# An attention and low-rank layer pair on one core: bulk loads behind the query stack, one-piece query split by way of DRAM, key copy and prologue on other engines

## The reference

```python
# x [2, 2048, 1024]; Wq, Wo [1024, 1024]; Wkv [1024, 64]; 32 heads of 32, one shared key/value head; float32
q  = (x @ Wq).reshape(b, s, 32, 32)
kv = x @ Wkv;  k, v = kv[..., :32], kv[..., 32:]
scores = einsum('bqhd,bkd->bhqk', q, k) * 32 ** -0.5
scores = where(causal, scores + slopes[:, None, None] * (pos_k - pos_q), -inf)      # ALiBi slopes
attn = einsum('bhqk,bkd->bqhd', softmax(scores), v).reshape(b, s, 1024) @ Wo
h = layernorm(x + attn)
# second layer: dense W [1024, 1024] and bias, plus a low-rank product whose rank (8, 16, 32 or 64)
# is that of the largest of four gate scores, taken row by row
out = layernorm(h + h @ W.T + bias + (h @ A[:r].T) @ B[:, :r].T)
```

## Time and profile before

| | |
|---|---|
| median of 3 runs | 3603.31 us (3599.54 to 3610.43) |
| the profiled execution | 3600.88 us, its span 3599.1 us |
| PE, DVE, ACT, POOL busy | 95%, 64%, 51%, 44% of the span |
| mean granted TensorE clock | 0.97 of full |
| DMA | 148.32 MB, mean 41 GB/s |

### The profile page before, as it was taken

One profiled execution on the slowest core, in us unless ns is written; L12 is line 12 of the kernel. 1 busy time (PEld: TensorE's weight loads), 2 busy tenths in 40 slices (PEclk: granted clock), 3 DMA queues, 4 the chain that ended last, 5 costly groups with the idle time before them and its releaser, 6 DMA issues. The chain is left out here.

```text
span 3599.1 us, 55753 instructions
## 1 busy us (share of the span) xinstructions
PE 3428.3 (95%) x20577; PEld 2225.1 (62%) x20577; DVE 2313.2 (64%) x5375; ACT 1822.1 (51%) x3188; POOL 1576.9 (44%) x467
## 2 busy tenths in 40 slices
PE   5989999999999999989999999999997999999998
PEld 3555555555555554555555555555544899999997
DVE  4657677777777772656777687777763455544454
ACT  2546656666676757536756666576765011101100
POOL 1114445665767766115536664768675001101010
PEclk8989999999999999989999999999998999999999
DMA  2221110101000100220110000000102112122121
GB/s 80 57 62 34 28 57 22 28 25 45 16 24 13 48 13 28 57 59 25 53 31 25 25 25 13 24 22 16 45 31 85 53 53 70 52 70 67 56 70 41
DMA packets 158395, 148.32 MB, mean 41 GB/s; under 512 B 9396, under 2 KB 141492, under 8 KB 156056
## 3 DMA queue, kind: packets, MB, share of 16 engines
q1 hardware_dynamic: 158168, 145.34, 13.6%
HBM read 94.39 MB, written 33.62 MB: 36 GB/s over the span
## 5 line engine op out<-in xcount | busy, mean ns | idle before, releaser
L931 ACT ACTIVATE prob<-ps_s,alibi 128x512 f32<-128x512 f32 (+3 forms) x2091 | 1236.7, 628 | 633.7 <-PE ps_s L1195 300.4
L1038 DVE TENSOR_REDUCE mxp<-ps_a 128x1 f32<-128x512 f32 x1536 | 974.0, 683 | 307.9 <-PE ps_a L1178 301.9
L882 POOL TENSOR_TENSOR prob<-prob 128x2048 f32<-128x2048 f32 (+1 forms) x240 | 1045.4, 4372 | 240.9 <-ACT prob L931 125.9
L1178 PE MATMUL ps_a<-wol,qst 97*128 97x512 f32 (+3 forms) x2560 | 971.9, 400 | 47.1 <-DVE mxp L1038 17.9
L1192 PE MATMUL ps_s<-qst,kexp 97*128 97x512 f32 (+3 forms) x2091 | 815.9, 394 | 25.7 <-DMA qst<-shift_t 14.6
L1041 DVE CUSTOM_DVE_ANT_0 ps_a<-ps_a,maska 128x128 f32<-128x128 f32 (+3 forms) x1024 | 486.5, 512 | 302.3 <-PE ps_a L1178 288.7
L1145 PE MATMUL ps_m<-woh,wol 128*128 128x512 f32 x1728 | 670.7, 423 | 9.7 <-DVE qst L1027 5.1
L1178 PEld LDWEIGHTS ps_a<-wol,qst 97*128 97x128 f32 x2560 | 494.6, 196 | 209.5 <-DVE mxp L1038 74.2
L1192 PEld LDWEIGHTS ps_s<-qst,kexp 97*128 97x128 f32 x2091 | 403.7, 193 | 301.7 <-ACT prob L931 151.1
L1201 PE MATMUL ps_o<-prob,val 128*32 128x512 f32 (+3 forms) x5120 | 574.7, 546 | 13.8 <-ACT prob L931 7.2
L867 POOL TENSOR_TENSOR wol<-wq_raw,wol 128x1024 fp32r<-128x1024 f32 x64 | 152.2, 2378 | 792.0 <-ACT wol L910 792.0
(11 more groups left out here) (125 smaller groups left out, 3645.3 us busy)
## 6 DMA issues: line engine op xcount, KB each, us to landing
wq_raw<-in_L_attn_Wq SPq DMA_DIRECT2D x64, 512.0 KB, 4.0
work<-in_L_attn_hidden_states SPq DMA_DIRECT2D x8, 2048.0 KB, 8.1
qst<-qst SPq DMA_DIRECT2D x64, 256.0 KB, 2.9
att_scratch<-at_sb SPq DMA_DIRECT2D x64, 256.0 KB, 2.3
at_raw<-att_scratch SPq DMA_DIRECT2D x32, 512.0 KB, 5.5
...
```

What stands on the lines that cost most here:

```text
L882: nc.gpsimd.tensor_tensor(even[:, :, c1:], even[:, :, c1:], odd[:, :, c1:], ALU.add).then_inc(pair_done, 1)
L931: nc.scalar.activation(prob[slot_of(step)][:, h, c0:], bank[:, c0:], ACT.Exp, bias=alibi_of(g, h, k - full_tiles(g))).then_inc(e_done, 1)
L1038: nc.vector.tensor_reduce(top, ps, AX.X, ALU.max).then_inc(a_done, 1)
L1178: last = nc.tensor.matmul(bank[:, 0:cols], qst[g % 3][0:KR, h, t * P:(t + 1) * P], kmax[0:KR, ring(sg):ring(sg) + cols], start=True, stop= ...
```

## The change

- **Query.** One ACT copy and one DVE subtraction on 128 partitions write `q_hi` and `q_lo` (in `wol`, part 7). Two DMAs write them to a DRAM tensor `q_rows` ("QO"); three read them back as rows 0 to 31, 32 to 63 and 64 to 95 of `qst` ("QI").
- **Bulk loads.** x is loaded in four parts of 256 columns. A Wq load and an x part are issued right behind the second QI of a unit.
- **Keys.** The copy to `kmax` is made by ACT ("KC"). `turn_v` waits for the first two parts only and uses a bank of `ps_a`; `ps_m` is free after the third.
- **Splits.** ACT splits Wq and Wo in halves; Wo's low part is made by POOL instead of DVE.
- **Mask.** On the diagonal the mask matmul comes ahead of the score matmul.
- **Prologue.** x in parts; the key product in `ps_o`; the slope and distance tables later on DVE; the first shift row ahead of the second query's stack, and no x load there.
- The planner has one ring for all DMAs, and some other gaps.

```diff
@@ planner (class Order)
+    def moved(self, at, size, delay):          # one ring for all transfers
+        begin = max(self.ring, at)
+        self.ring = begin + size
+        return begin + delay
@@ do_q_high, do_q_low: one piece instead of GH = 4
+    def do_keep_q(self, at, g, part):
+        self.put("QO", g, part)
+        self.push(self.moved(at, 1100, 2400) + self.QI_GAP, self.do_stack_q, g, part)
+    def do_stack_q(self, at, g, part):
+        self.put("QI", g, part)
+        landed = self.moved(at, 2200 if part == 0 else 1100, 3800 if part == 0 else 2700)
+        if part == 1:
+            self.stack_at[g], self.stacked = landed, g
+            self.push(at + self.BULK_GAP, self.do_bulk)
+    def do_bulk(self, at):                     # a wq load first, else a quarter of the next x load
...
@@ do_kv_part
+        if part == 1:
+            self.v_from = done + 55
+        if part == 2:
+            self.bank_at[self.M_BANK], self.bank_of[self.M_BANK] = done, ("k", sg)
...
+            self.push(done + 33, self.do_k_copy, sg)
@@ SyncE's queue
+            def load_x(sg, part):
+                cols = slice(part * XCOLS, (part + 1) * XCOLS)
+                sp.dma_start(xs[:, :, cols], xb[sg][:, :, cols]).then_inc(x_in[part], 16)
-            def repeat_q(g):
-                buf = g % 3
-                sp.wait_ge(ql_done, START + GH * (g + 1))
-                sp.wait_ge(stack_in, START + 16 * g)
-                sp.dma_start(qst[buf][DH:2 * DH].bitcast(F32), qst[buf][0:DH].bitcast(F32)).then_inc(stack_in, 16)
+            def keep_q(g, part):
+                if part == 0:
+                    sp.wait_ge(qh_done, START + g + 1)
+                    sp.wait_ge(stack_in, START + 48 * max(0, g - 1))
+                    sp.dma_start(q_rows[g % 2, 0], q_hi.bitcast(F32)).then_inc(q_out[0], 16)
+                else:
+                    sp.wait_ge(ql_done, START + g + 1)
+                    sp.dma_start(q_rows[g % 2, 1], q_lo.bitcast(F32)).then_inc(q_out[1], 16)
+            def stack_q(g, part):
+                sp.wait_ge(q_out[part], START + 16 * (g + 1))
+                rows = q_rows[g % 2, part].rearrange("(h r) q -> r h q", r=DH)
+                if part == 0:
+                    sp.wait_ge(s_full, START + tiles_before(max(0, g - 2)))
+                    sp.wait_ge(stack_in, START + 48 * g)
+                    for r in range(2):
+                        sp.dma_start(qst[g % 3][r * DH:(r + 1) * DH].bitcast(F32), rows).then_inc(stack_in, 16)
+                else:
+                    sp.dma_start(qst[g % 3][2 * DH:3 * DH].bitcast(F32), rows).then_inc(stack_in, 16)
@@ GpSimd: Wo's low part, from VectorE, in halves
+            def split_wo(c, half):
+                pool.wait_ge(wo_hi, START + 2 * c + half + 1)
...
+                nc.gpsimd.tensor_tensor(wol[:, c, cols], xs[:, c % QT, cols], woh[:, c, cols].bitcast(F32),
+                                        ALU.subtract).then_inc(wo_lo, 1)
@@ ScalarE: the query in one piece; the key copy, from VectorE; Wq and Wo in halves
+            def take_q(g):
+                act.wait_ge(q_ps, START + g + 1)
+                act.wait_ge(q_out[0], START + 16 * g)
+                nc.scalar.activation(q_hi, ps_m[:], ACT.Copy, scale=SCALE).then_inc(qh_done, 1)
+            def copy_k(sg):
+                cols = slice(ring(sg), ring(sg) + QB)
+                act.wait_ge(kv_lo, START + 2 * (sg + 1))
+                nc.scalar.activation(kmax[0:3 * DH, cols], kexp[0:3 * DH, cols].bitcast(F32),
+                                     ACT.Copy).then_inc(kv_done, 1)
@@ VectorE
-                nc.vector.scalar_tensor_tensor(qst[g % 3][2 * DH:3 * DH, h], ps_m[h * DH:(h + 1) * DH], SCALE,
-                                               qst[g % 3][0:DH, h].bitcast(F32), ALU.mult,
+                nc.vector.scalar_tensor_tensor(q_lo, ps_m[:], SCALE, q_hi.bitcast(F32), ALU.mult,
                                                ALU.subtract).then_inc(ql_done, 1)
@@ TensorE
-            def turn_v(sg):
-                pe.wait_ge(kv_done, START + sg + 1)
+            def turn_v(sg, bank):
+                pe.wait_ge(kv_hi, START + 2 * (sg + 1))
@@ scores_for_max, i == 0
-                    pe.wait_ge(stack_in, START + 16 * (g + 1))
+                    pe.wait_ge(stack_in, START + 48 * (g + 1))
+                    pe.wait_ge(kv_done, START + seg_of(g) + 1)
@@ scores
+                if diagonal:
+                    nc.tensor.matmul(bank[:, c0:c0 + P], identb[:], maskt[:], start=True, stop=False,
+                                     skip_group_check=True)
                 last = nc.tensor.matmul(bank[:, c0:], kexp[0:KR, at:at + P], qst[g % 3][0:KR, h, c0:],
-                                        start=True, stop=not diagonal)
-                if diagonal:
-                    last = nc.tensor.matmul(bank[:, c0:c0 + P], identb[:], maskt[:], start=False, stop=True)
+                                        start=not diagonal, stop=True, skip_group_check=True)
@@ prologue on SyncE
-            for g in range(2):
-                put_slopes(g)
-                load_wq(g + 1)
-                repeat_q(g)
-            load_x(1, DC)
+            put_slopes(0)
+            load_wq(1)
+            for part in range(2):
+                keep_q(0, part)
...
             put_shift(0, FIRST - 1)
```

388 lines of the change are left out of this document (225 added, 163 removed).

## The result

The changed kernel takes 3513.51 us (3511.45 to 3514.24, 4 runs), the kernel before beside it 3602.96: a ratio of 0.975, with a 95% interval of 0.973 to 0.976. The profiled execution after has a span of 3509.7 us at a mean clock of 0.98.

A forecast was written before the change was run, and what follows sets the result against it. PE was taken as the bound, busy 3428.3 of 3599.1 us, so only idle time, lower clock and matmul spacing could be won. Terms of -17 -22 -12 +8 -7 -10 +13 +5 sum to -42, giving 3560 us, range 3525 to 3592.

The forecast's parts named there:

- Prologue -17: Chain to the first score tile: shorter waits for x, V's transposes, maxima and shift row, -17 us (-10 to -20).
- Key copies -22: PE's waits before V's transposes, for DVE copies held by POOL additions, go in four later segments: idle 11.7, clock 10.
- Wo's split -12: Two places where PE waits for a maximum behind a DVE split piece: twice 3.5 us idle and 2.5 clock.
- end of the attention +8: Split halves moved to POOL lengthen its unbroken additions and follow the last division: +8 us (0 to 13).
- Shift row behind x -7: At 205.42 PE waited 4.62 us for a shift row issued behind the third segment's x; with clock, -7 us.
- Mask first +13: Diagonal matmul order: 256 narrow tiles cost 0.05 to 0.06 us more each, +13 us; bounds -8 and +28.
- Short units -10: Two DVE-bound spells in short units: fewer subtractions save 4 us each plus 1 of clock, -10 us (0 to -24).
- stack +5: Query stack through DRAM takes longer, which PE feels in the 16 short units: +5 us; bounds -8 and +64.
- The rule of the two hops: Skill page: two dependent DMAs pay the fixed 2 us twice; on 16 short units, +32 us instead of +5.
- the attention's time per long unit changes: Sign that would show the prediction wrong: a changed attention time per long unit, which no term touches.
- The rival of the planner's new waits: The newly laid list gives PE other waits; prologue's 17 and half the held-copy gain stay: 3590 to 3597, chance 0.13.
- 41 / 5: Number of short units with late stacks, given as about 9, from which the kernel is slower than before.

The follow-up runs named there:

- the best lists found of the two forms: Changed kernel with the query in four pieces and the planner's gaps reset: 3515.47 us; changed kernel, query in one piece, four planner numbers changed: 3477.98 us.
- the best list found for each form: Kernel before with three planner numbers changed: 3549.07 us (0.9874); changed kernel with four planner numbers changed: 3477.98 us (0.9672).

## Why the prediction was wrong

The sign and most mechanisms were right; the size was off by 47 us. By its own steps:

- **Prologue -17**: -17.9 to the first exponential, and the first score tile where it was forecast. Right in sum. Two steps that the term didn't have cancelled: the first stack came 1.9 us later by way of DRAM, and the first query product took 5.6 us instead of 7.35, at full clock.
- **Key copies -22**: 25 alone on the old list. Right in size, but 15 of it was clock, some of that a stretch behind a run of max tiles. In the changed kernel the copy's engine is worth nothing, since no copy on VectorE began while a POOL addition ran there.
- **Wo's split -12 and end of the attention +8**: 10 and 7, measured together in the changed kernel. Right. The forecast had the end at +8; it is +7.2, of which 3.8 is idle time and 3.3 the cost of the lower clock, and that varies by as much between kernels.
- **Shift row behind x -7**: 5 to 10, not clear of noise. The wait that was named did fall, from 4.62 us to 0.91, but it does so with whole x loads too, so the list or the order of issue did that.
- **Mask first +13**: wrong in sign. It is 0 to -6, since the masks right behind PV were left to a bound ("-8") instead of being counted. 13 to 19 us of the miss.
- **Short units -10, stack +5**: the query edit was given 5 net and is worth 15 to 37. The sentence that failed is "Elsewhere the 3 x 64 pieces less on each of the two engines are hidden behind PE and are worth nothing". Between the best lists found of the two forms, 18 us lie in the short units and 25 in the long ones, with 4 given back in the prologue. The stack by DRAM is waited for in the prologue and hardly after it (1.9 us at 61, 0.9 us at 1442), near the low bound. The rule of the two hops (estimate +32) did not come true in the time, although the second hop was longer than assumed, 3.9 us; where nothing hid the stack, in the prologue, it came 1.9 us later, as the rule has it.
- **The list itself: no term.** This is the step that was missing. The text said "the whole list is laid out anew" and priced only new waits, upwards. It also said that the prediction is wrong "if the attention's time per long unit changes (no term touches it)", and there a part of the miss lies: units 16 to 31 and 40 to 63 gained 48 us, where three of the four held copies and Wo's split promised about 28. The list's order alone moved one or the other kernel by 12 to 49 us. It does so through small waits and the clock behind them, some of it at runs of max tiles, none of which shows in a table of waits above 0.8 us.
- **Two sums.** The rival of the planner's new waits doesn't follow from what it names: 3603 less 17 and less half of 22 is 3575, not 3590 to 3597, unless the +13 and +8 are added. And 41 / 5 is 8, not 9. Neither bears on the forecast.

How the 89 us (91 by the ratio) divide can only be bounded. On the best list found for each form, the kernel before stands at 0.987 of its time and the changed one at 0.967, so the edits are worth about 2.0%, 73 us, and the other 18 are that the kernel before had drawn a list 45 us worse than its best, and the changed one a list 27 worse than its own. "Best found" is not best, and how far each search went matters. Of the profiled spans' 71, 17 are in the prologue, 22 in the short units, 10 and 11 in units 8 to 15 and 40 to 47, 10 and 8 in units 16 to 31 and 48 to 63, less 7 given back at the end. In units 24 to 31 alone the difference is 13 us, 10 of them neither idle nor clock, but that is mostly work on the other side of the cut: PE does 2792 matmuls there instead of 2843, and 50 more in the stage before.

So the miss of 47 us is, by these bounds, 13 to 19 the mask, 10 to 32 the query (15 to 37 instead of 5) and some 18 the list. The parts overlap, and no run divides them more finely.
